# Weights of expert n requested when the additions of expert n-5 have landed, and the last group's shared expert done behind the 64 experts

## The reference

```python
xn  = layernorm(x)
out = x + attention(xn) + moe(xn)
# attention(xn): exp(xn @ (proj*ab).T - 0.5*|xn|^2*ab^2) for 512 features, times a 512x512 weight made in the same way
# moe(xn):
scores = sigmoid(xn @ router_w)            # 64 experts in 8 groups; best 4 groups, then top 8 experts
topk_w = 2.5 * topk_w / topk_w.sum()
# each expert takes its first 256 (CAP) tokens
y_e = (silu(X_e @ gate_w[e]) * (X_e @ up_w[e])) @ down_w[e]      # 512 -> 256 -> 512
out[token] += weight * y_e
out += (silu(xn @ sgate_w) * (xn @ sup_w)) @ sdown_w             # shared expert, every token
```

## Time and profile before

| | us |
|---|---|
| median of 3 executions | 1291.22 (1290.9 to 1291.5) |
| profiled execution, its own time | 1295.88 |
| profiled execution, span from first to last instruction | 1294.1 |

### The profile page before, as it was taken

The page is one execution under the profiler, slowest core; times in us unless marked ns, Lnnn a source line. Parts: engine busy times, 40 slices in busy tenths (PEclk is TensorE's granted clock), DMA queues, the critical chain, the costliest instruction groups (busy, mean ns, idle before and its releaser), DMA issues.

```text
span 1294.1 us, 23005 instructions
## 1 busy us (share of the span) xinstructions
PE 1269.8 (98%) x7577; PEld 1118.6 (86%) x7577; DVE 930.5 (72%) x1853; ACT 648.2 (50%) x1130; POOL 421.5 (33%) x344
## 2 busy tenths in 40 slices
PE   8999999999999999999999999999999999999993
PEld 7888888888888888888889999999999999999993
DVE  7887787867878678785655777777777777777771
ACT  6422223222232223322255777777777777777771
POOL 1000000000000000000013666666666667677753
PEclk9999999999999999999999999999999999999997
DMA  8246654575545755446447999999999999999995
GB/s 309 85 137 153 135 132 113 143 168 115 133 111 145 168 107 137 112 116 136 137 132 211 297 288 302 290 299 293 298 289 297 293 293 284 299 290 301 286 250 66
DMA packets 204777, 263.66 MB, mean 204 GB/s; under 512 B 41012, under 2 KB 131016, under 8 KB 204744
## 3 DMA queue, kind: packets, MB, share of 16 engines
q1 hardware_dynamic: 175272, 191.40, 51.5%
q0 software_dynamic: 28672, 71.32, 24.5%
q10 hardware_dynamic: 800, 0.53, 0.2%
HBM read 178.18 MB, written 71.39 MB: 193 GB/s over the span
## 4 chain that ended last, share of the span: by engine, by line
PE 91%; POOL 3%; issue 3%; DVE 1%; DMA 1%; ACT 0%; POOLq 0%; ACTq 0%
PE pmm L1344 17%; PE pmm L1343 17%; PE pmm L1342 16%; PE pout L1342 11%; PE pout L1344 11%; PE pout L1343 11%; PE ptr L1599 4%; PE plp L1407 2%; POOL out_dram L1758 2%; POOL xbuf L1748 1%; PE pmm L1617 1%; PE ptr L1354 1%; DMA out_dram<-xbuf,slot_cols 1%; PE plp L1436 1%; PE plp L1416 1%
## 5 line engine op out<-in xcount | busy, mean ns | idle before, releaser
L1344 PE MATMUL pmm<-xt_hi,proj_lo 128*128 128x256 f32 (+1 forms) x768 | 241.2, 314 | 0.0
L1343 PE MATMUL pmm<-xt_lo,proj_hi 128*128 128x256 f32 (+1 forms) x768 | 241.1, 314 | 0.0
L1344 PE MATMUL pmm<-xt_hi,sgu_lo 128*128 128x256 f32 (+1 forms) x764 | 240.1, 314 | 0.0
L1343 PE MATMUL pmm<-xt_lo,sgu_hi 128*128 128x256 f32 (+1 forms) x764 | 240.1, 314 | 0.0
L1342 PE MATMUL pmm<-xt_hi,proj_hi 128*128 128x256 f32 (+1 forms) x736 | 232.5, 316 | 0.0
L1342 PE MATMUL pmm<-xt_hi,sgu_hi 128*128 128x256 f32 (+1 forms) x732 | 231.3, 316 | 0.0
L1742 POOL TENSOR_TENSOR earlier<-earlier,chosen 128x64 bf16<-128x64 bf16 x64 | 24.2, 378 | 611.4 <-DVE chosen L976 607.7
L1748 POOL DMA_INDIRECT xbuf<-rows,slot_cols x128 | 165.6, 1294 | 85.7 <-issue 37.4
L569 ACT ACTIVATE feat<-pmm,ab 128x512 f32<-128x512 f32 x66 | 45.4, 689 | 286.4 <-PE pmm L1344 286.4
L1343 PEld LDWEIGHTS pmm<-xt_lo,proj_hi 128*128 128x128 f32 x768 | 144.2, 188 | 11.2
L1343 PEld LDWEIGHTS pmm<-xt_lo,sgu_hi 128*128 128x128 f32 x764 | 143.4, 188 | 11.2
(11 more groups left out here) (220 smaller groups left out, 2640.1 us busy)
## 6 DMA issues: line engine op xcount, KB each, us to landing
raw<-in_L_ffn_gate_w_dram SPq DMA_DIRECT2D x64, 512.0 KB
raw<-in_L_ffn_up_w_dram SPq DMA_DIRECT2D x64, 512.0 KB
raw<-in_L_ffn_down_w_dram SPq DMA_DIRECT2D x64, 512.0 KB
outs<-in_L_attn_x_dram SPq DMA_DIRECT2D x32, 512.0 KB, 3.7
out_dram<-outs SPq DMA_DIRECT2D x32, 512.0 KB, 3.1
xbuf<-in_L_attn_x_dram SPq DMA_DIRECT2D x52, 256.0 KB, 8.1
raw<-xn SPq DMA_DIRECT2D x52, 256.0 KB, 6.5
rows<-raw SPq DMA_DIRECT2D x39, 256.0 KB, 4.8
```

The source lines that it names most:

```text
L1343: pe.matmul(psum, lh, rl, start=False, stop=False)
L1344: ins = pe.matmul(psum, ll, rh, start=False, stop=final and n == len(pairs) - 1)
```

## The change

There are two parts.

*Weights.* SP's refill of expert n now first waits for `added` to show that the additions of experts 0 to n-5 have landed. The order of its requests is gate(n), down(n-2), up(n). Before it was gate(n), up(n), down(n-1), with no such wait.

*Shared expert of the last group.* `last_group` no longer does the shared expert: TensorE has 48 + 24 products of 128x512 fewer there. It does `count` first, and the attention products in pieces (`attention_part`) between which the look-up stands. On SP the load of the residual goes behind the first `load_chunk`. The 512 tokens of the last group become experts 64 and 65 (256 rows each), with the shared weights, behind the 64 experts: their normalised rows are loaded by SP from the DRAM table instead of gathered, and there is no addition by indirect DMA. In their place, when all additions have landed, SP loads the last group's 512 rows of `out` into `xn` (two loads of 512 KB), VectorE adds the results (four of 128x512), and SP stores them (two stores of 512 KB).

```diff
+SHARED_PARTS = GROUP // CAP
+LAST = E + SHARED_PARTS
@@ sync
-            load_residual(turn(GROUPS - 1))
             for b in range(2):
                 sp.wait_ge(counts_stored[b], 32 * GROUPS // 2)
             load_chunk(0)
+            load_residual(turn(GROUPS - 1))
...
+            def load_last_rows(e):
+                sp.wait_ge(slot_w_made, e.n - 1)
+                for c in range(CB):
+                    j = CB * (e.n - E) + c
+                    sp.dma_start(xe[e.b][:, c, 0:H], rows_groups[GROUPS - 1][:, j, 0:H]).then_inc(
+                        last_rows_loaded[e.n - E], 16)
+            def merge_last_rows(a):
+                sp.dma_start(xn[:, 2 * a:2 * a + 2, :], out_halves[GROUPS - 1, a]).then_inc(rows_back[a], 16)
+            def store_last_rows(a):
+                sp.wait_ge(merged[a], CB)
+                sp.dma_start(out_halves[GROUPS - 1, a], outs[a][:]).then_inc(out_stored[a], 16)
+            def refill(e, gate=None, up=None):
+                at_least(sp, added, 16 * CB * e.prev().prev().prev().prev().n)
+                refill_half(e, 0, gate_w[e.n] if gate is None else gate)
+                refill_down(e.prev().prev())
+                refill_half(e, 1, up_w[e.n] if up is None else up)
...
-            for n in range(E - 2 * CHUNK, E):
-                refill_gate_up(turn(n))
-                refill_down(turn(n - 1))
-            refill_down(turn(E - 1))
+            for n in range(E - 2 * CHUNK, E):
+                refill(turn(n))
+            for n in range(E, LAST):
+                refill(turn(n), sgate_w, sup_w)
+                load_last_rows(turn(n))
+            for n in range(E, LAST):
+                refill_down(turn(n), sdown_w)
             sp.wait_ge(added, 16 * CB * E)
+            for half in range(2):
+                merge_last_rows(half)
+            for half in range(2):
+                store_last_rows(half)
@@ scalar
+            def last_group(g):
+                for r in range(HB - 1):
+                    features(1 + g.n, r, feat_hi)
+                sum_signs(0)
+                features(1 + g.n, HB - 1, feat_hi)
+                gate_up_hi(turn(0))
+                act.wait_ge(up_done, IB * (GROUPS - 1))
+                gate_up_hi(turn(1))
...
             e_turned_hi(turn(0))
+            sum_signs(1)
@@ vector
             def last_group(g, base):
+                count(g)
                 features_lo(1 + g.n, 0, feat_hi, feat_lo)
...
+                features_lo(1 + g.n, 1, feat_hi, feat_lo)
                 pass_blocks(0)
+                features_lo(1 + g.n, 2, feat_hi, feat_lo)
                 slot_tokens(0)
+                features_lo(1 + g.n, 3, feat_hi, feat_lo)
+                output(g, 0)
+                output(g, 1)
+                gate_up_lo(turn(0), (0,))
                 pass_blocks(1)
+                gate_up_lo(turn(0), (1,))
                 output(g, 2)
@@ vector, last
+            def merge(a, c):
+                e = turn(E + a)
+                dve.wait_ge(rows_back[a], 16)
+                if e.n < LAST - 1:
+                    dve.wait_ge(e_out_made, CB * e.n + c + 1)
+                    source = outs[a][:, c, :]
+                else:
+                    dve.wait_ge(down_done, CB * e.n + c + 1)
+                    source = pout[c]
+                dve.tensor_tensor(outs[a][:, c, :], source, xn[:, CB * a + c, :], ALU.add).then_inc(merged[a], 1)
@@ tensor
             def last_group(g):
-                dense_dots(g, (0, 1))
                 count(g)
-                dense_dots(g, (2, 3))
-                for m in range(2):
-                    shared_products(g, 0, m)
+                dense_dots(g, (0, 1, 2))
+                attention_part(g, 0, (0, 1))
                 pe.wait_ge(logits_summed, GROUPS)
                 look_up(0)
-                attention(g, 0)
-                for m in range(2):
-                    shared_products(g, 1, m)
-                attention(g, 1)
-                shared_down(g, 0)
-                shared_down(g, 1)
+                dense_dots(g, (3,))
+                attention_part(g, 1, (0, 1))
+                attention_part(g, 0, (2,))
+                attention_part(g, 1, (2,))
+                attention_part(g, 0, (3,))
+                attention_part(g, 1, (3,))
+                attention_part(g, 2, range(HB))
                 look_up(1)
-                output(g, 2)
...
-            output(turn(GROUPS - 1), 3)
+            attention_part(turn(GROUPS - 1), 3, range(HB))
```

More of the change, by code:

```diff
@@ L313, in build @@
         gathered = [sem(f"gathered{b}") for b in range(2)]
+        last_rows_loaded = [sem(f"last_rows_loaded{a}") for a in range(2)]
         slot_w_made = sem("slot_w_made")
@@ L330, in build @@
         added = sem("added")
+        rows_back = [sem(f"rows_back{a}") for a in range(2)]
+        merged = [sem(f"merged{a}") for a in range(2)]
         x_groups = x.rearrange("b s h -> (b s) h").rearrange("(g j p) h -> g p j h", j=J, p=P)
@@ L541, in refill_down @@
+            def refill_down(e, source=None):
                 sp.wait_ge(edn_hi_made, e.n - 1)
                 sp.wait_ge(edn_lo_made, e.n - 1)
[L543 to L547, removed]
+                load_down(e.b, down_w[e.n] if source is None else source)
+            def load_last_rows(e):
[4 more added lines that the diff above has]
+                        last_rows_loaded[e.n - E], 16)
@@ L548, in _ @@
+            refill_half(turn(3), 0, gate_w[3])
+            refill_half(turn(3), 1, up_w[3])
+            for k in range(CHUNK):
+                refill(turn(CHUNK + k))
+                if k == 1:
+                    load_chunk(3)
+            with sp.Fori(1, CHUNKS - 3) as m:
                 for k in range(CHUNK):
-                    e = Turn(2 * m + 2 + k // 2, k % 2, k // 2)
-                    refill_gate_up(e)
-                    refill_down(e.prev())
+                    refill(Turn(2 * m + 2 + k // 2, k % 2, k // 2))
@@ L657, in gate_up_hi, with group @@
                                    egu_raw[e.b][:, at], copy).then_inc(egu_hi_made[m], 1)
-            def group(g, last=False):
+            def group(g):
                 nxt = g.next()
@@ L746, in _ @@
             group(turn(GROUPS - 2))
-            group(turn(GROUPS - 1), last=True)
+            last_group(turn(GROUPS - 1))
             def down_hi(e):
@@ L1593, in e_turn @@
             def e_turn(e):
-                pe.wait_ge(gathered[e.b], 16 * CB * (e.i + 1))
+                if isinstance(e.n, int) and e.n >= E:
+                    pe.wait_ge(last_rows_loaded[e.n - E], 16 * CB)
+                else:
+                    pe.wait_ge(gathered[e.b], 16 * CB * (e.i + 1))
                 at_least(pe, e_xt_lo_made, 2 * e.n)
@@ L1670, in _ @@
                     e_down(e.prev())
-            for n in range(E - 6, E - 2):
+            for n in range(E - 6, LAST - 2):
                 e_gate_up(turn(n))
```

135 lines of the change are left out of this document (63 added, 72 removed).

## The result

The changed kernel takes 1364.4 us (median of 4 runs, 1363.7 to 1367.7), the kernel before on the same chip 1291.4 (4 runs, 1290.9 to 1293.4): a ratio of 1.057, 95% interval 1.0555 to 1.0582. It is 73 us slower. The prediction was 1282.6 in a range of 1278 to 1297, and faster with 70 in 100. The second rival came true, close to its far end (at a period of 10.6 us its 80 us on top of 1282.6 make 1362.6).

What follows compares the result with a forecast made beforehand. TensorE's work, then late additions, were taken to bound the kernel. -14.0 (passage) + 18.4 (two stages) - 20.0 (old tail) + 7.0 (new tail) = -8.6 from the 1291.2 median gave 1282.6 us, range 1278 to 1297.

Steps and rivals of the forecast that it cites:

- The second rival: Weights' wait holds TensorE up in some 58 stages; slower above a 9.37 us period, 80 us at 10.6; 24 in 100.
- What bounds the kernel: Whole span: TensorE's work to 1274 us, then the late additions worked off behind it, to 1294.1.
- the tail: Behind TensorE's end in the kernel before: 20.0 us in which only additions run.
- the arrears: Delay from an expert's first copy to its addition: 4.0 us (expert 8) to 11.0 (expert 63), forecast about 2.5.
- TensorE's balance: Shared expert moved: 72 products removed (16.3 us), two stages of 9.22 added (18.4), so +2.1 us if nothing waits.
- The passage: From the routing's counts to expert 0: turning at 666.0 instead of 679.2, experts' stages 14.0 us earlier.
- The rival of a passage that shows: Before expert 0, TensorE waits for chunk and gather and gains only 8 us: time 1288.6, 9 in 100.
- The new tail: After the last addition, landing at 1275.5: reload, VectorE's additions and store take 10.0 us, ending at 1285.5.
- I take 0 for its cost: SP's wait in front of the weights: costs 0 us, the later requests fitting their slack of 8.8 and 5.8.
- withheld weights leave the DMA engines to the additions: At SP's wait: additions profit and start about 2.5 us behind the copy instead of 4 to 11.
- Does the wait bind?: At SP's request for gate(n): with additions 4.0 us behind, the request comes 7.0 us later, within 15.8 of slack.
- The rival of additions that land no sooner: Chain of additions keeps its 9.3 us period and ends at 1280.1: span 1290.1, time 1287.2, 15 in 100.

Runs made afterwards that it cites:

- moved, new order: Shared expert moved and requests ordered gate(n), down(n-2), up(n) as in the changed kernel, but without the wait for additions: median 1285.5 us.
- burst without wait: The changed kernel without the wait for additions, all three weights requested together when up(n) may be, at TensorE's pace: 1285.7 us (one run).
- looser waits: The changed kernel with its landing wait on expert n-6 instead of n-5, or only in front of up(n): 1344.9 and 1323.8 us.
- small burst: The changed kernel with its landing wait, but only a quarter of gate and up loaded, 0.75 MB instead of 1.5: 1286.5 us (one run).
- The wait for an issue: The changed kernel, but SP waits until GpSimd has issued the additions of n-5, not for their landing: 1285.2 us, ratio 0.9939.

## Why the prediction was wrong

- *What bounds the kernel, the tail, the arrears.* Right in the main. The arrears are a matter of the additions' chain and of the load, but also of when in a stage the weights are requested, which I hadn't looked at: at the same load the new order takes them to 1.9 us.
- *TensorE's balance.* Right: in "moved, new order" stages are 9.22 and TensorE ends at 1276.4, which is 1274.05 - 16.0 + 18.4.
- *The passage.* Forecast -14.0 with bounds of 16.3 and 8; measured -16.0. The second look-up and the turning follow each other without a wait, at 664.1 and 664.6, where I had 666.0: the row numbers were ready at 657.0 and the gather issued at 657.50, 0.6 us earlier than I had it, and the turning wasn't held up by the second look-up. That is 14.6 us earlier than 679.2, and the six shared products behind it give the other 1.4; the 0.6 us that I had for ScalarE's signs between the turnings weren't paid. The rival of a passage that shows is out.
- *The new tail.* Right in kind. In "moved, new order" the last addition starts at 1265.5, 2.6 us before the 1268.1 of the forecast, and the reload is requested at 1272.60; the span ends 9.5 us later (10.0 forecast). Against this kernel my span of 1285.5 is 3.4 us too long (its span is 1282.1) and my time of 1282.6 is 2.9 too short (its median is 1285.5): the profiled execution of before, with its own time of 1295.9, was 4.7 us above the median of its runs, and I took that difference off; this kernel's profiled execution (1283.9) was 1.6 us below its own median.
- ***"I take 0 for its cost", "withheld weights leave the DMA engines to the additions"*. This is the step that failed.** It costs 1364.4 - 1285.5 = 79 us. I compared the slack of a request (8.8 and 5.8 us) with the weights' own time (3.2 us for two), as if the wait only shifted the request. I had seen that the weights would start at the landing of n-5, thus together with addition n-4, and put it into the rival, but in the forecast I let the addition profit: the engines would be its own until the weights come. In truth they come at the same moment, all 1.5 MB of them, and go first. The trace of before has the price at hand: 1.57 MB are 4.8 us of full DMA time, and an addition alone has a period of 7.34. Overlap of the addition's way to its first packet (2.1 us when it runs alone) with the burst leaves 4.8 - 2.1 = 2.7, and 7.34 + 2.7 = 10.0, above the 9.37 from which I had the kernel slower. Measured is 10.5. The price of the burst was too low: at a share of 1.00 it went at 286 GB/s, so 1.57 MB take 5.5 us and not 4.8; with that the sum is 10.7.
- *Does the wait bind?* Even with additions in time it does: in "moved, new order" they start 1.9 us behind the copy and land 8.3 later, at 10.2, and gate(n) is requested at 6.6 (6.2 for expert 62 in the earlier trace rows). I had counted that as 7 us of slack used up, and didn't see that a wait that always binds makes the start of every burst an event of the chain itself.
- *The rival's sign and size.* "At the 10.6 seen once it would be 80 us": measured are 10.5 us, and 82 us over the forecast (1364.4 - 1282.6). I gave it 24 in 100 with its weight on the mild end. The argument against it ("if the period is less the chain catches up") assumed that the period can be less; with the wait it can't, since the burst is tied to each landing.
- *The rival of additions that land no sooner* leaned on a rule of the Trainium skill, "DMA: Bandwidth & Descriptors", section "Queues, rings and completion order": turns between the queues, packet by packet. The trace of the changed kernel doesn't show it for an addition whose packets would begin while a burst drains: q1 alone for 4.5 us, then q0. It does show for indirect transfers that were issued before the burst: in "burst without wait", from 908.5 to 912.5, q0 has 22.7% beside q1's 77.3%, and all its packets are those of gathers issued before the burst (their rows are 4.6 KB, the addition's 2 KB). So by these runs what was issued ahead of a burst gets turns in it, and an addition issued with it doesn't get them at once. Why was not tried.

What stays open: whether the addition's packets wait in the making of their descriptors or in the engines' queues; and what causes the slow issues (2.5 us instead of 1.6) that turn the looser waits. On these the traces have a hint: in "moved, new order" 14 of the 15 issues over 2 us are the second issue of every fourth expert, each beside VectorE's `past` and the conversion right behind it; this is a coincidence in time that no run tried. That the burst alone doesn't cost is shown by the burst without the wait (1285.7), that the landing wait alone doesn't by the small burst (1286.5), the latter at a lower total load. The wait for an issue (1285.2) is the lowest median, 0.6% below the kernel before, but level with the kernel that has no wait (1285.5), whose requests it makes nearly at the same times.

## What to carry to other kernels

Before you make a load wait for a landing, ask what else that landing releases. If both the load and the next link of a chain start on it, the load is ahead in every link, and its full DMA time, less the link's own start-up, goes into the chain's period (here 2.7 us by the estimate above, 2.9 by the packets); compare the new period with the stage, not the load's slack with its own duration. A loop closed like this doesn't recover from a disturbance when the period with the burst is longer than the stage: if the wait binds only now and then, one late transfer makes it bind for good. Where loads must be throttled, tie them to progress outside the chain, and look first at the order of requests, which here gave by itself what the wait was to give.

## What the runs showed of the hardware

- A burst of three plain loads (1.5 MB) kept the 16 DMA engines at a share of 1.00 for 4.5 us, and an indirect addition issued with it had its first packet 5.0 us after its issue (median), against 2.3 where the loads came behind it and 2.1 with no load at all.
- A DMA share above 0.9 hid a serial chain. 0.94 at 258 GB/s and 1.04 at 291 to 295 GB/s are both digits of 9 on the page, 13 to 14% apart in bytes; only the windows' GB/s tells them apart.
- An addition's issue on GpSimd took 1.6 us, and 2 to 3 us in some: in 15 of 128 in "moved, new order", 59 of 128 with the small burst.
- After TensorE had stood for 3.9 us, its granted clock was 0.53 over the next 5 us, and products of 128x512 started 0.42 us apart instead of 0.23. Over the experts' half (660 us, mean clock 0.97) this cost 20 us at most, beside 53 us of standing.
